# Rounding the output banks of the last block: first half by VectorE inside a pair, second half by ScalarE

## The reference

```python
def _qdot(x, w, out_dtype=BF16):
    return jnp.dot(x.astype(E4M3), w.astype(E4M3), preferred_element_type=out_dtype)
ff_gate = _qdot(x, w_gating[0])
gate_value = jax.nn.gelu(ff_gate)
ff1 = _qdot(x, w_gating[1])
activations = gate_value * ff1
outputs = _qdot(activations, w_linear)
...
x = x + _L1_ffn_ref(_layernorm(x, axis=-1), L1_ffn_w_gating, L1_ffn_w_linear)
```

## Time and profile before

| | us |
|---|---|
| median of 3 runs | 722.06 |
| lowest and highest run | 721.88, 723.37 |
| the profiled execution | 722.73 |
| its span, first to last instruction | 720.9 |
| busy in the span: PE, DVE, ACT, POOL | 660.1, 548.9, 479.7, 436.0 |
| mean granted TensorE clock, of full | 0.990 |

### The profile page before, as it was taken

The page is one execution under the profiler, slowest core; times in us unless marked ns, Lnnn a source line. Parts: engine busy times, 40 slices in busy tenths (PEclk is TensorE's granted clock), DMA queues, the critical chain, the costliest instruction groups (busy, mean ns, idle before and its releaser), DMA issues.

```text
span 720.9 us, 16231 instructions
## 1 busy us (share of the span) xinstructions
PE 660.1 (92%) x5782; PEld 527.8 (73%) x5782; DVE 548.9 (76%) x1180; ACT 479.7 (67%) x982; POOL 436.0 (60%) x618
## 2 busy tenths in 40 slices
PE   2789999988899999999999999999999999999784
PEld 1567777667788877888888888888888888876442
DVE  3699999999787877676777676676767766766887
ACT  1577877756466576666666666666666666658994
POOL 2378878878877545565656656665656554464500
PEclk9999999999999999999999999999999999999997
DMA  8200003203201000000000100000100000000001
GB/s 282 77 9 9 10 9 117 70 1 106 86 1 38 15 1 2 15 30 9 23 24 17 28 9 25 23 16 16 31 9 16 15 1 3 1 1 1 31 29 60
DMA packets 26019, 22.83 MB, mean 32 GB/s; under 512 B 5041, under 2 KB 24402, under 8 KB 25810
## 3 DMA queue, kind: packets, MB, share of 16 engines
q1 hardware_dynamic: 24160, 20.92, 9.2%
q10 hardware_dynamic: 1778, 0.86, 0.4%
HBM read 19.67 MB, written 2.10 MB: 30 GB/s over the span
## 4 chain that ended last, share of the span: by engine, by line
POOL 38%; issue 26%; PE 15%; DVE 14%; ACT 3%; ACTq 1%; POOLq 1%; DVEq 0%
POOL rstd L734 14%; POOL pr L702 5%; POOL p_n L709 5%; PE banks L1594 2%; POOL w L725 2%; POOL w_raw L722 2%; PE banks L1613 2%; PE banks L1614 2%; DVE h_sum L1093 2%; DVE hid_b L1086 2%; POOL var L732 1%; POOL qk_norm L644 1%; DVE h_magic_b L1091 1%; DVE half L852 1%; POOL hid_lo L671 1%
## 5 line engine op out<-in xcount | busy, mean ns | idle before, releaser
L734 POOL TENSOR_TENSOR rstd<-var,minus_half 128x8 f32<-128x8 f32 x64 | 106.1, 1657 | 5.0
L709 POOL TENSOR_TENSOR p_n<-pr,pinv 128x256 f32<-128x256 f32 x64 | 39.3, 614 | 75.7 <-DVE pinv L1001 75.7
L702 POOL TENSOR_TENSOR pr<-pr,rstd 128x256 f32<-128x256 f32 x63 | 38.6, 613 | 74.1 <-DVE pr L1011 74.0
L1316 ACT ACTIVATE kT<-banks,gk_q 128x512 f32<-128x512 f32 x64 | 44.0, 688 | 49.1 <-PE banks L1755 49.1
L1745 PE MATMUL banks<-m_hi,z_hi 128*128 128x256 f32 x256 | 74.9, 293 | 0.7 <-DVE z_lo L992 0.6
L1745 PE MATMUL banks<-m_hi,z_lo 128*128 128x256 f32 x256 | 72.3, 283 | 0.0
L1745 PE MATMUL banks<-m_lo,z_hi 128*128 128x256 f32 x256 | 72.3, 282 | 0.0
L992 DVE TENSOR_TENSOR z_lo<-banks,z_hi 128x512 fp32r<-128x512 f32 x64 | 43.9, 686 | 29.1 <-ACT z_hi L1301 29.0
L1039 DVE TENSOR_REDUCE sums<-q_sq 128x4 f32<-128x512 f32 x64 | 43.7, 683 | 25.2 <-ACT q_sq L1340 25.2
L1362 ACT ACTIVATE qT<-banks 128x512 f32<-128x512 f32 x64 | 38.2, 597 | 32.9 <-PE banks L1849 32.9
L1007 DVE TENSOR_REDUCE pmax<-banks 128x4 f32<-128x256 f32 x64 | 27.0, 422 | 41.1 <-PE banks L1776 41.0
(11 more groups left out here) (194 smaller groups left out, 2059.2 us busy)
## 6 DMA issues: line engine op xcount, KB each, us to landing
w_raw<-in_L_xattn_Wq SPq DMA_DIRECT2D x4, 512.0 KB, 5.8
wo_raw<-in_L_xattn_Wo SPq DMA_DIRECT2D x1, 2048.0 KB, 9.2
k_ctx<-in_ctx SPq DMA_DIRECT2D x16, 128.0 KB, 2.7
w_raw<-in_L_ffn_w_gating SPq DMA_DIRECT2D x16, 128.0 KB, 2.3
out_x<-x_sb SPq DMA_DIRECT2D x4, 512.0 KB, 2.9
x_sb<-in_x SPq DMA_DIRECT2D x1, 1536.0 KB, 9.3
a_ctx<-in_ctx SPq DMA_DIRECT2D x16, 64.0 KB, 1.8
w_raw<-in_L_xattn_Wk SPq DMA_DIRECT2D x2, 512.0 KB, 9.1
```

Of the source, the lines that this page charges most:

```text
L702: pool.tensor_tensor(pr[:, u % 2, :, :], pr[:, u % 2, :, :], roots_of[:, HC:2 * HC].unsqueeze(2).to_broadcast([P, HC, S]), ALU.mult).then_ ...
L709: pool.tensor_tensor(p_n[:, u % 2, :, :], pr[:, u % 2, :, :], pinv[:, u % 2, :].unsqueeze(2).to_broadcast([P, HC, S]), ALU.mult).then_inc( ...
L734: pool.tensor_tensor(rstd1[:, par, :], var1[:, :], minus_half[:, :].to_broadcast([P, 2 * HC]), ALU.pow).then_inc(root1, 1)
L1316: act.activation(kT[u % 2][:, :, :].rearrange("p h n -> p (h n)"), bank[2][:, :], ACT.Copy, scale=gk_q[:, :]).then_inc(kT_ready, 1)
```

## The change

A group's first half (bank 4) is rounded by VectorE, its second half (bank 5) still by ScalarE. For groups 0, 1 and 2 VectorE's cast stands inside the pair v = 5, 9 or 13, between `h_magic_b` and `h_sum`; for group 3 it stands behind group 2's additions. Each half has its own semaphore, and `down8` of a group's first step waits for both.

```diff
+            def rounded_first(g):
+
+                dve.wait_ge(d_down_done, J1 * (g + 1))
+                after(dve, d_updated, GT * (g - 1) + 2)
+                dve.tensor_copy(y_b[:, 0, :, :].rearrange("p r n -> p (r n)"), bank[4][:, :]).then_inc(d_rounded_first, 1)
+
-            def hidden8(u, n):
+            def hidden8(u, n, first_of=None):
...
                 dve.tensor_scalar(h_magic_b[:, two, :], h_pow[:, two, :], E4M3_LEAST, E4M3_IN_BF16, ALU.max, ALU.mult).then_inc(h_steps, n)
+                if first_of is not None:
+                    rounded_first(first_of)
                 dve.wait_ge(h_steps, 3 * u + 2 * n)
                 dve.tensor_tensor(h_sum[:, two, :], hid_b[:, two, :], h_magic_b[:, two, :], ALU.add).then_inc(h_steps, n)
...
-                    dve.wait_ge(d_rounded_y, 2 * g + b + 1)
+                    dve.wait_ge(d_rounded_second if b else d_rounded_first, g + 1)
...
-                hidden8(2 * v, 2)
+                hidden8(2 * v, 2, v // PAIRS - 1 if v % PAIRS == 1 and v > PAIRS else None)
...
             group_output8(NG - 2)
+            rounded_first(NG - 1)
             group_output8(NG - 1)
...
-                for b in range(2):
-                    after(act, d_updated, GT * (g - 1) + 2 * (b + 1))
-                    act.activation(y_b[:, b, :, :].rearrange("p r n -> p (r n)"), bank[4 + b][:, :], ACT.Copy).then_inc(d_rounded_y, 1)
+                after(act, d_updated, GT * g)
+                act.activation(y_b[:, 1, :, :].rearrange("p r n -> p (r n)"), bank[5][:, :], ACT.Copy).then_inc(d_rounded_second, 1)
...
                 if j == 0:
-                    after(pe, d_rounded_y, 2 * g)
+                    after(pe, d_rounded_first, g)
+                    after(pe, d_rounded_second, g)
```

More of the change, by code:

```diff
@@ L372, in build @@
         h_steps = sem("h_steps")
-        d_rounded_y, d_updated = sem("d_rounded_y"), sem("d_updated")
+        d_rounded_first, d_rounded_second, d_updated = sem("d_rounded_first"), sem("d_rounded_second"), sem("d_updated")
         k_bank = (bank[1], bank[7])
```

## The result

The changed kernel takes **724.88 us** (median of 7 runs, 724.62 to 727.34) against 722.09 us (7 runs) for the kernel before beside it: ratio 1.0036, 95% interval 1.0021 to 1.0051, so 2.6 us longer. The profiled execution took 725.40 us, its span is 723.6 us.

What follows compares the result with a forecast made beforehand. VectorE was taken to bound the last stage, waiting for no other engine. Casts in the pairs +1.36 us and tail +0.1 us gave +1.45 us, 723.5 us on the runs' scale; range 722.3 to 725.1 us.

Steps and rivals of the forecast that it cites:

- the side called slower: Whole kernel: above the border of 723.5 us, chance 0.50, of which 0.20 for TensorE's stop reaching VectorE.
- The sum: Whole kernel: casts in the pairs +1.36 us and tail +0.1 us, together +1.45 us.
- The cast's price, 0.42 us: VectorE in the pairs: each cast stretches h_magic_b to h_sum from 0.53 to 0.95 us.
- the second rival: VectorE in the pairs: bank copies run fast, each cast costs 0.16 us, +0.3 us in all, 722.4; chance 0.14.
- the sum of 1.9 us: VectorE: alternative total if each operation waits for the pipe to empty, about 0.6 us a cast; the prediction argued against it.
- The first cast, 0.42 + 0.1: VectorE, v = 5: the cast's 0.42 us plus 0.1 us for falling beside GpSimd's d_xhat.
- TensorE's stops: First down projections in v = 6, 10, 14: TensorE waits for the cast, standing still 2.2 to 2.4 us more.
- The sum takes 0 for this: Pairs after the casts: TensorE's stops are hidden from VectorE, so they add 0 us.
- The cover of 0.6 us: v = 11, the tightest place: the gelu, delayed by TensorE's stop, still ends 0.6 us before VectorE wants it.
- the first rival: TensorE's stop lowers the granted clock; 1.1 us reach VectorE at v = 11, +1 to +3 us more; chance 0.20.
- The tail, 0.1 us: Last group: VectorE casts after group 2's additions, so its additions start 0.1 us later than before.

Runs made afterwards that it cites:

- wait_only: Kernel before, ScalarE rounding everything, but TensorE's first down projection of groups 1 to 3 also waits for h_sum of v = 5, 9 or 13; ratio 1.0038.
- fill: Changed kernel plus eight unused 128x512 matmuls ahead of the down projections of v = 6, 10 and 14, filling TensorE's stops; ratio 1.0017 to the kernel before.
- one_cast: Changed kernel with only group 1's cast (v = 9) on VectorE, ScalarE rounding the rest; ratio 1.0017 to the kernel before.
- end_fill: Kernel before plus eight unused 128x512 matmuls ahead of its last four down projections; ratio 0.9995.
- late_two: Changed kernel with only the casts of groups 1 and 2 (v = 9 and 13) on VectorE; ratio 1.0010 to the kernel before.
- tail_only: Changed kernel with only group 3's first half cast by VectorE, ScalarE rounding groups 0 to 2; ratio 1.0007 to the kernel before.
- small_ops: Kernel before plus three 128x16 VectorE memsets at the places of the casts in the pairs, with the same two waits ahead of each; ratio 1.0008.
- change_again: The changed kernel, unaltered, timed once more in a later set; ratio 1.0023 to the kernel before.
- three_casts: Changed kernel without the tail's cast: VectorE casts at v = 5, 9 and 13, ScalarE rounds both halves of group 3; ratio 1.0016 to the kernel before.
- early_two: Changed kernel with only the casts of groups 0 and 1 (v = 5 and 9) on VectorE; ratio 1.0018 to the kernel before.
- wait_fill: wait_only plus eight unused 128x512 matmuls in each of TensorE's three stops; ratio 1.0000 to the kernel before.

## Why the prediction was right on the sign and short by one rival

The measured 724.88 us lies in the range (722.3 to 725.1), on the side called slower, but 1.4 us above the forecast. The sum was 1.45 us, the stage grew by 2.47, and the median lies 0.2 us inside the upper end, which was put there for a rival that the sum left out. So the sign was forecast by its mechanism, the place in the range was in part luck. Point by point:

- **The cast's price, 0.42 us: right.** `h_magic_b` to `h_sum` is 0.94 us (691.61 to 692.55) where 0.95 was forecast, and the pairs v = 9 and 13 are longer by 0.39 or 0.40 us in all kernels with a cast there. The nearest row, the bank addition, was the right one; the cheap cast, the second rival, is out with 683 ns. The Trainium skill, "VectorE: DVE Perf Modes", section "Why PSUM operands drop a tier", had ruled it out too: the trace agrees, 683 ns for 512 elements is no faster than the fp32 addition. Its section "The DRAIN you can't avoid" would have each operation start after the one before has ended; the cast starts 0.34 us after the start of a 0.43 us row, so the sum of 1.9 us that followed from it was too much. The section itself goes on that a next operation "that is not held starts earlier", which agrees with this row and which the prediction left out.
- **The first cast, 0.42 + 0.1: mis-sized.** It holds VectorE as said (676.44 to 677.54, 1.10 instead of 0.68 us), but `h_sum` behind it took 0.68 instead of the 0.85 us of the earlier trace rows, and the pair is 0.01 us shorter. The next pair, v = 6, is 0.18 longer. Both together are 0.17, not 0.52 us. wait_only has the stop of TensorE without the cast: there v = 5 is 0.24 shorter and v = 6 0.25 longer, so the stop moves time from one pair to the next at no cost in sum, and the 0.17 is the cast's. GpSimd's `d_xhat`, beside which VectorE's rows are longer, moves in the same way: its second half now waits for TensorE's transposes and ends later. The first row is of before, the others of after:

```profile
674.28 7.42 POOL L757 TENSOR_SCALAR d_xhat<-x_sb,row_stats,row_rstd 128x256 f32<-128x256 f32 x4 [4.37 <-PE banks L1712]
674.49 3.62 POOL L757 TENSOR_SCALAR d_xhat<-x_sb,row_stats,row_rstd 128x256 f32<-128x256 f32 x2 [4.37 <-PE banks L1720]
680.15 3.11 POOL L757 TENSOR_SCALAR d_xhat<-x_sb,row_stats,row_rstd 128x256 f32<-128x256 f32 x2 [2.04 <-PE banks L1720]
```

That this is what moves VectorE's time was not tried. So the casts in the pairs come to 0.95 instead of 1.36 us.
- **TensorE's stops: right in size.** Forecast 2.4, 2.3 and 0.46 + 2.2; measured 2.47, 2.32 and 2.76 us.
- **"The sum takes 0 for this": the step that failed.** The cover of 0.6 us was sized rightly (0.64 in fill), but it holds at full clock only. The reason for a full clock was one row of one execution, the stop of 2.18 us at 683.62 without a fall. In three of the experiments' profiles (one_cast, end_fill, late_two) that same stop was followed by a fall, in three others (before, tail_only, small_ops) it wasn't; of the fifteen unfilled stops of 2.31 to 2.95 us at v = 6, 10 and 14, seven were followed by one. So one row without a fall was no ground for a full clock. What the first rival described is what happened, in its own numbers: the queued work ended 1.7 us later than at full clock (697.60 against 695.55 plus the 0.36 by which `h_magic_b` comes later after), and 1.03 us reached VectorE at v = 11, forecast 1.1. It had been given 0.20. Of the profiles of kernels with unfilled stops at both v = 6 and v = 10 (after, change_again, wait_only, three_casts, early_two), all five have exactly one fall that reached VectorE, which then waited 0.66 to 1.50 us; of the nine others none. That is one profile each.
- **The tail, 0.1 us: right in the profiled execution**, 5.21 against 5.11, with the last down projection at half clock in both. But the new tail hangs on VectorE, not on the clock: it is 5.19 to 5.21 whether that projection takes 0.61 us (fill, change_again) or 1.03 (after, tail_only), while ScalarE's is 4.69 at full clock. Where an execution ends at full clock, the cast at the end costs 0.5 us. That was not foreseen.
- **The 0.37 us ahead of `hid` in v = 14: in no step of the prediction.** Nothing in the profile of before points to it.

The terms as measured are 0.95 for the casts, 1.03 for the clock, 0.37 for the wait in v = 14 and 0.10 for the tail: 2.45 of the stage's 2.47 us. The forecast had 1.36 + 0.1. Too much for the casts (0.41) and nothing for the last wait (0.37) nearly cancel, by luck; the clock is the rest.

How much of this is in the median of the runs is less sure. The first `hid_b` of the last block starts between 654.08 and 658.34 us of the fourteen profiled spans, though no experiment changed what runs before it, so the times carry a scatter from elsewhere that is larger than the effect. The changed kernel was 2.6 us longer in the result above and 0.23% = 1.7 us in change_again, without the clock's wait (fill) it was 1.2 us, and these intervals overlap. That the stops cost time in the runs, not only in single profiles, is shown by wait_only against wait_fill alone.

## What to carry to other kernels

A wait that is moved onto a busy engine's queue can be hidden in every row and still cost time, because TensorE, once it has stood still, may resume at half clock: ask of the cover whether it still holds when the work behind the stop takes twice as long, and take for the clock more than one execution, since the same stop falls or doesn't from one to the next. Where one engine sets the pace, as VectorE does here, the price of an operation added to it was read from the nearest row of the same shape and memory (0.42 us forecast, 0.39 measured); the start-to-start distance of rows (0.60 us behind a cast), not their length (0.69), is what it holds the engine for.

## What the runs showed of the hardware that was not expected

- **Three tiny instructions can cost 0.4 us on an engine that is otherwise full**: in the profile of small_ops three memsets of 0.07 us bring a wait of 0.38 us some fifty operations after the first of them, and two casts bring none (early_two, late_two). Its times (1.0008 [0.9997, 1.0019]) can't tell it from no change.
- **Where the clock falls changes from execution to execution of one kernel.** The changed kernel had it after v = 10 once and after v = 6 and in v = 14 the other time, not necessarily on the same chip; on one chip, the mean granted clock of one_cast's eleven runs went from 0.982 to 0.991. A fall in v = 8 (one_cast, end_fill, late_two) made VectorE wait for nothing; after v = 6 or v = 10 it waited 0.66 to 1.50 us in all five cases.
- **Doing unused matmuls is cheaper than standing still**: 24 of them turned a ratio of 1.0038 into 1.0000 in the kernel without casts. In the changed kernel (1.0036 and 1.0023, filled 1.0017) the intervals overlap.
- **ScalarE's rows grow when it works off a backlog, its pace doesn't.** Behind the starved stretch its copies start every 0.48 us while a row's length climbs from 0.61 to 0.73 us, so there the distance of the starts, not the length of a row, tells its cost:

```profile
699.18 0.61 ACT L1382 ACTIVATE gate_b<-banks 128x512 bf16<-128x512 f32 x1
699.65 0.62 ACT L1387 ACTIVATE up_b<-banks 128x512 bf16<-128x512 f32 x1
...
706.32 0.72 ACT L1382 ACTIVATE gate_b<-banks 128x512 bf16<-128x512 f32 x1
706.80 0.73 ACT L1387 ACTIVATE up_b<-banks 128x512 bf16<-128x512 f32 x1
```
